# A graph network on one core: the first pass's register loads of slot numbers, in fours behind copies on ScalarE and in eights behind counts on TensorE

## The reference, cut to what matters

```python
h = jnp.maximum(_layernorm(x, axis=-1), 0.0)             # x: 6250 nodes x 128
h = _gcn_conv(h, src, dst, ones_e, W1, b1, n)            # 106250 edges, sorted by dst
h = h / jnp.maximum(jnp.sqrt(jnp.sum(h * h, axis=-1, keepdims=True)), 1e-12)
ev = _edge_encoder(h, src, dst, We1, be1)                # sigmoid(h[src] @ We[:H] + h[dst] @ We[H:] + be)
na = _node_encoder(h, src, dst, ev, Wn1, bn1, n)         # relu(segment_sum(ev * h[src], dst) @ Wn + bn)
ev2 = _edge_encoder(na, src, dst, We2, be2)
g = _node_encoder(na, src, dst, ev2, Wn1, bn1, n)
x = x + _gcn_conv(g, src, dst, ev2, W2, b2, n)
```

## Time and profile before

| | us |
|---|---|
| median of 3 runs | 3329.52 (3324.85 to 3332.83) |
| the profiled execution, its own time | 3348.71 |
| its span, first to last instruction | 3346.9 |
| first pass, from its first strip copy to the last | 143.3 to 977.1 |
| of it: before the first flush | 143.3 to 163 |
| of it: first stage, 27 turns, counts and pairs | 163 to 534 |
| of it: second stage, counts, pairs and pieces | 534 to 980 |
| TensorE's mean granted clock | 0.924 of full |

### The profile page before, as it was taken

The page is one execution under the profiler, slowest core; times in us unless marked ns, Lnnn a source line. Parts: engine busy times, 40 slices in busy tenths (PEclk is TensorE's granted clock), DMA queues, the critical chain, the costliest instruction groups (busy, mean ns, idle before and its releaser), DMA issues.

```text
span 3346.9 us, 58780 instructions
## 1 busy us (share of the span) xinstructions
PE 2635.7 (79%) x16470; PEld 2291.0 (68%) x16470; DVE 2111.6 (63%) x6199; ACT 1617.9 (48%) x3249; POOL 1866.2 (56%) x1816
## 2 busy tenths in 40 slices
PE   0667667898997677777789899999999676777775
PEld 0344446888885667666678788888888566666665
DVE  5567676665635566666675567666676456666667
ACT  7256565666666454554454444444444422233232
POOL 5345456555405666667720666666661267776673
PEclk9788898999999898988899899999999888888998
DMA  4244445555542333333322444444442433333333
GB/s 114 80 147 152 147 155 192 193 208 211 189 174 78 100 100 106 107 98 114 99 71 79 124 134 135 135 135 135 134 134 81 141 98 97 107 106 100 112 99 94
DMA packets 185594, 419.58 MB, mean 125 GB/s; under 512 B 36655, under 2 KB 136700, under 8 KB 175533
## 3 DMA queue, kind: packets, MB, share of 16 engines
q10 hardware_dynamic: 83703, 244.23, 20.6%
q0 software_dynamic: 61472, 140.49, 15.3%
q1 hardware_dynamic: 40118, 31.23, 3.0%
HBM read 311.35 MB, written 102.16 MB: 124 GB/s over the span
## 4 chain that ended last, share of the span: by engine, by line
PE 67%; issue 13%; DVE 9%; ACT 3%; ACTq 3%; another core or an unknown queue 2%; DMA 1%; DVEq 1%; POOL 1%; SPq 0%; POOLq 0%
PE ps L1117 18%; PE ps_high L1109 16%; PE ps_high L1117 12%; PE ps L1057 7%; PE ps_high L1075 3%; PE ps L1041 3%; ACT tab_area L769 2%; PE ps_high L1070 2%; ACTq L377 1%; PE ps_high L1196 1%; DVE acc L1592 1%; DVE tab_area L1521 1%; PE ps L1229 1%; DVE weights L1568 1%
## 5 line engine op out<-in xcount | busy, mean ns | idle before, releaser
L601 POOL DMA_INDIRECT rows<-table,edge_src x1664 | 1759.9, 1058 | 1164.0 <-SPq L496 604.0
L1109 PE MATMUL ps_high<-rows,weights 128*128 x2784 | 648.0, 342 | 385.2 <-issue 235.6
L1117 PE MATMUL ps<-tab_area,acc 128*128 128x129 f32 (+2 forms) x4410 | 824.2, 327 | 7.4 <-issue 6.1
L1109 PEld LDWEIGHTS ps_high<-rows,weights 128*128 128x128 f32 x2784 | 473.6, 204 | 486.9 <-issue 292.9
L1117 PEld LDWEIGHTS ps<-tab_area,acc 128*128 128x128 f32 x4410 | 698.6, 206 | 52.3 <-issue 7.2
L863 ACT ACTIVATE step<-xbuf,rows 128x128 f32 x928 | 358.0, 394 | 690.4 <-PE ps_high L1109 312.8
L1592 DVE TENSOR_TENSOR acc<-acc 128x640 f32<-128x640 f32 x735 | 604.9, 823 | 102.3 <-ACT acc L872 64.7
L1117 PE MATMUL ps_high<-tab_area,acc 128*128 128x129 f32 (+2 forms) x2940 | 588.3, 326 | 0.3 <-issue 0.3
L1575 DVE TENSOR_TENSOR acc<-acc,ps_high 128x129 f32 (+1 forms) x948 | 335.1, 354 | 384.9 <-PE ps_high L1109 187.8
L769 ACT ACTIVATE tab_area<-ps_high x816 | 404.4, 496 | 304.9 <-PE ps_high L1075 178.7
L1117 PEld LDWEIGHTS ps_high<-tab_area,acc 128*128 128x128 f32 x2940 | 478.0, 206 | 29.8 <-issue 1.2
(11 more groups left out here) (242 smaller groups left out, 2177.8 us busy)
## 6 DMA issues: line engine op xcount, KB each, us to landing
acc<-counts ACTq DMA_DIRECT2D x105, 1120.0 KB
counts<-tab_area ACTq DMA_DIRECT2D x51, 1568.0 KB
acc<-counts ACTq DMA_DIRECT2D x25, 1568.0 KB
rows<-table,edge_src POOLq DMA_INDIRECT x1664
table<-tab_area SPq DMA_DIRECT2D x6, 903.0 KB, 4.8
table<-acc SPq DMA_DIRECT2D x7, 448.0 KB, 4.2
table<-tab_area SPq DMA_DIRECT2D x6, 455.0 KB, 3.9
table<-tab_area SPq DMA_DIRECT2D x6, 448.0 KB, 3.0
```

What stands on the lines that cost most here:

```text
L601: nc.gpsimd.indirect_dma_start(rows[:, t % UNROLL, 0:row_floats[k]], None, tables[k], bass.IndirectOffsetOnAxis(ap=edge_src[:, t:t + 1], a ...
L1109: nc.tensor.matmul(ps[DENSE_BANKS + m % PAIR_BANKS][:, 0:WIDTH[k]], weights[:, m % W_RING, :], rows[:, bass.ds(known["slots"][m % UNROLL], ...
L1117: ins = nc.tensor.matmul(ps[j][:, 0:WIDTH[k]], gate_blocks[:, n % S_RING, j * PART:(j + 1) * PART], table[:, h, 0:WIDTH[k]], start=(h == 0 ...
```

## The change

ScalarE no longer loads 16 + 16 slot numbers at a flush. It loads 4 numbers of `done_from` behind the copy of each slot m with m % 4 = 0, and 4 of `count_to` behind that of m % 4 = 1, for the group of four slots that follows. The two numbers of a flush are loaded one behind the copy of the turn's slot 10 and one behind that of slot 11. At the flush itself only the wait for the last copy, the wait for the flush before and the DMA are left. TensorE loads 8 + 8 numbers in two instructions, one behind the counts of the third slot of each eight and one behind those of the seventh, for the next eight slots. The values, the copies, the matmuls and the DMAs are the same.

```diff
-        def load_slots(engine, table, i, top):
+        def load_some(engine, table, i, n, top):
             return nc.values_load_multi_w_load_instructions(
-                table[0:1, i * UNROLL:(i + 1) * UNROLL], engines=[engine], min_val=0, max_val=top,
+                table[0:1, i * n:(i + 1) * n], engines=[engine], min_val=0, max_val=top,
...
-            def slot_places(i):
-                return (load_slots(SCA, done_from, i, (REGIONS - 1) * REGION),
-                        load_slots(SCA, count_to, i, (C_RING - 1) * C_TILE // WINDOW + FLUSH - 1))
-
-            done_at, count_at = slot_places(0)
+            def load_done(i):
+                return load_some(SCA, done_from, i, QUAD, (REGIONS - 1) * REGION)
+
+            def load_count(i):
+                return load_some(SCA, count_to, i, QUAD, (C_RING - 1) * C_TILE // WINDOW + FLUSH - 1)
+
+            def load_flush(j, part, top):
+                return nc.values_load_multi_w_load_instructions(
+                    flush_to[0:1, j, part:part + 1], engines=[SCA], min_val=0, max_val=top,
+                    skip_runtime_bounds_check_because="a place in the ring and a tile")[1][0]
+
+            done_at, count_at = load_done(0), load_count(0)
             for m in range(QUAD * TURNS):
                 if m < SLOTS:
...
                     ins.then_inc(cells_copied, 1)
+
+                    if m % QUAD == 0 and m + QUAD < SLOTS:
+                        next_done = load_done(m // QUAD + 1)
+                    if m % QUAD == 1 and m + QUAD < SLOTS:
+                        next_count = load_count(m // QUAD + 1)
+                    if m % QUAD == QUAD - 1:
+                        done_at, count_at = next_done, next_count
+                    if m % FLUSH == FLUSH - 6:
+                        ring = load_flush(m // FLUSH, 0, C_RING - 1)
+                    if m % FLUSH == FLUSH - 5:
+                        tile = load_flush(m // FLUSH, 1, DENSE_TILES)
                     if m % FLUSH == FLUSH - 1:
                         j = m // FLUSH
-                        ring, tile = (nc.values_load_multi_w_load_instructions(
-                            flush_to[0:1, j, part:part + 1], engines=[SCA], min_val=0, max_val=top,
-                            skip_runtime_bounds_check_because="a place in the ring and a tile")[1][0] for part, top in ((0, C_RING - 1), (1, DENSE_TILES)))
-                        if m + 1 < SLOTS:
-                            done_at, count_at = slot_places(j + 1)
                         act.wait_ge(cells_copied, m + 1)
...
                 def count(m):
                     u, b = m % (2 * QUAD), m // QUAD
                     if u == 0:
-                        at = load_slots(TEN, cell_turns, m // (2 * QUAD), (REGIONS - 1) * REGION)
-                        first_pass.cell_at, first_pass.zero_at = at[:2 * QUAD], at[2 * QUAD:]
+                        first_pass.cell_at, first_pass.zero_at = first_pass.cells_next, first_pass.zeros_next
...
+                    if u == QUAD // 2 and m + 2 * QUAD < SLOTS:
+                        first_pass.cells_next = load_turn(2 * (m // (2 * QUAD) + 1))
+                    if u == QUAD + QUAD // 2 and m + 2 * QUAD < SLOTS:
+                        first_pass.zeros_next = load_turn(2 * (m // (2 * QUAD) + 1) + 1)
+
+                def load_turn(i):
+                    return load_some(TEN, cell_turns, i, 2 * QUAD, (REGIONS - 1) * REGION)
...
                 pe.wait_ge(ld_slot_rows, 16 * 6)
+                first_pass.cells_next, first_pass.zeros_next = load_turn(0), load_turn(1)
```

More of the change, by code:

```diff
@@ L768, in _ @@
                         act.wait_ge(cells_done, m)
[L769 to L770 removed]
+                    ins = act.activation(c_cells[:, bass.ds(count_at[m % QUAD], NODE_TILES, step=PART // WINDOW), :],
+                                         ps_high[:, bass.ds(done_at[m % QUAD], CELLS)].rearrange("p (h d) -> p h d", d=WINDOW), ACT.Copy)
                     if m > 0:
```

2 lines of the change are left out of this document (removed).

## The result

The changed kernel takes 3307.64 us (median of 5 runs, 3297.96 to 3309.3) where the kernel before takes 3329.52 (5 runs, 3324.85 to 3334.41): a ratio of 0.9932, with a 95% interval of 0.9916 to 0.9949. It is faster, by 22 us and not by the 47 that were forecast. The profiled execution took 3307.64 us, with a span of 3305.8 and a mean granted clock of 0.929. The profiled execution of before had been 19 us over its median, so the two spans differ by 41 us, of which 21 us lie behind the first pass, where nothing was changed.

The account below looks back on a forecast made before the run. ScalarE's flush stop was taken to hold up the first stage, TensorE to bound the second. Gains of 43 us (first stage), 2 (flush ahead) and 2 (second stage) summed to 47, giving 3282.5 us, range 3256 to 3313.

Parts of the forecast that it names:

- what bounds: First stage: no engine near full, waits in turns, ScalarE's flush stop among them; second stage: TensorE's own.
- the flush: ScalarE's stop at each flush falls from 2.96 to 0.75 us, 2.21 us shorter.
- what is late next: First stage: ScalarE's need nears VectorE's and TensorE's, so coupling waits don't shrink; 328 us, 43 less than 371.
- ScalarE's loads: New loads behind ScalarE's copies: four numbers take 0.43 us; uncovered 0.5 us a turn, plus 0.4 for flush traffic.
- the straight line: Price of a register load drawn between one and sixteen numbers, 0.049 us a number: four in a row 0.43 us.
- TensorE's loads: Two loads of eight at 0.66 us each fit under queued work; 8 us of first-stage stops go.
- The second stage gives 1 to 3 us: Second stage: small gain from clears waiting behind ScalarE's copies (2.0 us) and from issue (0.6 us).
- VectorE and the pairs take over: Rival: ScalarE's gain turns into TensorE's waits at groups VectorE marks late; gain 20 us, 3309.5 us; chance 0.20.
- The clock comes back too: Rival: fewer stops also restore part of TensorE's clock; gain about 70 us, 3259.5 us; chance 0.18.
- Short loads are not short: Rival: four in a row cost 1.00 us like four apart, so the kernel gets slower, 3410 us; chance 0.08.
- Nothing comes of it: Rival: the loads slow each other and use up the gain, within 7 us of before; chance 0.04.
- The signs named in advance: Checks on stop, load times, copy spacing, first stage about 45 us earlier, clock, and a chain without ScalarE's slot loads.

Follow-up runs that it names:

- c1: The kernel before, with waits against loaded numbers turned into waits against constants, but for one in sixteen: 0.9998 of the kernel before.
- c2: The whole change, with the same constant waits as c1: 0.9929 of the kernel before.
- d1: c1 with ScalarE loading in fours behind copies in the first stage only, TensorE's loads as before: 0.9863 of the kernel before.
- c3: c2 with TensorE's loads put back as before, so ScalarE's part of the change alone: 0.9905 of the kernel before.
- c4: c1 with TensorE's two loads of eight only, ScalarE's loads as before: 1.0018 of the kernel before.
- f1: The whole change, plus TensorE's and VectorE's pair loads split into fours and ones: 0.9888 of the kernel before.
- e2: ScalarE's part of the change, plus TensorE's and VectorE's pair loads split into fours and ones: 0.9817 of the kernel before.
- d2: c1 with ScalarE loading in fours behind copies in the second stage only, TensorE's loads as before: 1.0042 of the kernel before.
- d4: c3 without L371, TensorE's load of four numbers that lie four apart: 0.9760 of the kernel before.
- d3: c1 without L371, TensorE's load of four numbers that lie four apart: 0.9939 of the kernel before.
- e1: c3 with the four numbers of TensorE's load L371 copied once to neighbouring places: 0.9838 of the kernel before.
- f3: e2 with TensorE's slot numbers loaded in fours too: 0.9839 of the kernel before.
- e3: c3 with TensorE's 16 slot numbers still in one load, but behind the counts of each eight's seventh slot: 0.9952 of the kernel before.

## Why the prediction was right and wrong, by its steps

**The account in the sum's own terms**, before and after, by the two traces: ahead of the first stage 3 us came of the 2 forecast, in the first stage 26 of 43, and in the second 9 us were lost where 2 were to be gained. Together the pass ends 20 us earlier and not 47. In c1 and c2 the same terms are 4, 40 and a loss of 18. Which of the two stages missed more hangs on the pair of traces, but both missed.

**Right: what bounds, and the flush.** ScalarE's stop was on the path of the first stage. It fell from 2.96 to 0.68 us (forecast 0.75), and the change in the first stage by itself gave 44 us of the whole time (d1), where the sum had 43 for it and 2 for the flush ahead of it. The step "what is late next" held in its main point, that the waits which couple three nearly equal engines would not shrink.

**Mis-sized: ScalarE's loads.** Quiet they took 0.312 us and not 0.43. The cover was there. Before, the flush's first load began at 459.65 and the stop of 2.96 us ahead of the copy at 462.78 only at 459.82, so 0.17 of its 0.28 us ran under the last copy; behind each of the three loads lay a gap of 0.02 to 0.04 us. After, in the first stage, the copy behind a load of four under 0.4 us starts 0.528 us after the one before (median of 149), behind a load of one number (0.279 us) 0.528 (54), and with no load between 0.529 (162). So the uncovered 0.5 us a turn are zero. In the wake they took 0.9 to 1.1 us; 67 of the 216 in the first stage took over 0.4. The copy behind such a load follows in 1.06 us in the median (0.88 to 1.2 for the middle half), so 0.35 to 0.7 us each, 2.5 a turn: some 1.3 us a turn where I had 0.4. Both terms together were 0.9 and came out as 1.3, some 10 us over the stage. The prediction had the right reading at hand, "pieces of some 0.25 us, each holding a few neighbours", and chose the straight line beside it. By pieces the load of 16 pair numbers at 3.604 us is four pieces of 0.9 us, and the price of one piece in a wake could have been read before the result.

**Wrong: TensorE's loads.** The step said that a load of eight would be covered by what is queued, and that 8 us of stops would go. They did not. Of ScalarE's 120.8 us of idle time in the first stage after, 20.5 are the flush stops and some 35 the loads in a wake; the other waits are some 65 us, as much as the 63.5 before and not 8 less. With the loads in the wake that makes 20 us over the sum; 4 us less elsewhere leave the 16 by which 344 us lie over the 328 worked out (c2 and c3 had 332 and 333, from 372). In the whole time the part seems to cost 6 to 8 us (c3, c4, at the edge of noise), and 24 us where nothing else is long (f1 against e2, clear of it). The loads of 16 had stood at slots 0 and 8 of a turn. In the first stage 21 of those 54 were slow before; in the second stage one of 45. The "behind counts" of the change puts them to slots 2, 6, 10 and 14, and in the second stage 23 of 90 are slow (over 1.2 times the median). I had looked at what is queued ahead of a load and not at when in a turn it runs.

**Wrong: the second stage.** "The second stage gives 1 to 3 us" was the step that failed in its sign. It was right that nobody waits there for ScalarE's stop. But the stop also set when the flush's DMA goes out. With the stop, that DMA went out 1.8 us behind the last copy in this stage (2.5 us in the first); now it is 0.2 us. So in five of the 23 turns TensorE's pair loads, which had mostly begun just ahead of the flush, now run in its wake: in the kernel after L371 takes 2.6 to 3.7 us there where it mostly had 1.0, and with ScalarE's part alone (c3) L365 takes 4.0 to 4.2 and L371 another 1.5. The stage is 14 us longer in c3, 10 us when it alone is changed (d2, 13 us of the whole time), and 1 us with L371 gone (d4 against d3). In c3 half of the 14 us is TensorE standing longer (45.7 us against 38.9) and half is more busy time for the same work at a lower clock (395.4 against 388.2, 0.96 against 0.99). That the DMA's earlier issue moved the loads into the wake is read from the order in the traces; no run moved the DMA alone. The prediction noted L365 at 3.604 us, priced it for ScalarE's own loads, and didn't ask which of the loads that stay would meet the flush after the change. It also took TensorE's loads in this stage as covered, by the 0.6 us of "issue" ahead of the pieces. The pairs' matmuls, which stand behind the pair loads, already stood for 11.7 us there:

```profile
L1041 PE MATMUL ps<-rows,weights 128*128 x524 | 104.7, 282 | 25.2 <-issue 11.7 <-DVE weights L1500 10.7 <-DVE xbuf L1507 2.1
```

**Of the rivals**, none was the one. "VectorE and the pairs take over" has the time (3309.5 us forecast, 3307.64 measured) and one of its signs: VectorE's lines have 21% of the chain of the first stage, shown below, where they had 12%. Its mechanism isn't what was measured: ScalarE's other waits did not grow, in d1, with the same VectorE, the first stage keeps 38 us, and the loss of the second stage goes with one load. "The clock comes back too" came in a small part, 0.90 for 0.87 in the first stage, and was seen once L371 was gone or the pair loads were short: 0.97 in d4 and e2. The quarter of the stage at half clock, which its sum uses, no run shows as such; it is an estimate from the mean. The traces give the clock as a share of full speed: in that of before it was 0.50 from 464 to 467, behind that flush, and 1.00 from 468 to 470, and with these two levels a mean of 0.87 is 0.26 of the time at 0.50; the 0.90 of after is 0.20. "Short loads are not short" is refuted for quiet loads by the 0.312 us; in the wake, with 0.9 to 1.1, it holds for a third of those of the first stage. "Nothing comes of it" is out, as the gain is clear of noise. The chain of the first stage after:

```profile
by line: issue 16.4%; PE ps_high L1082 15.9%; PE ps_high L1087 15.0%; PE ps L1054 14.7%; ACT tab_area L776 10.0%; DVE tab_area L1541 9.1%; DVE tab_area L1538 4.8%; DVE xbuf L1527 4.5%; DVE weights L1520 2.8%; ACTq L377 2.7%; DVEq L365 1.2%;
```

**The signs named in advance:** ScalarE's stop, the loads of 0.3 us and of 0.5 to 0.7 for eight, the copies 0.53 us apart, the clock of the first stage and VectorE's share of the chain came as named. The first stage ended 29 us earlier and not 45, and the chain still holds ScalarE's loads, for 2.7% of the stage where it was 9.3%. The two that were named for failure both came: loads in the wake of 0.8 us or more on ScalarE, and a second stage that moves by more than 5 us.

## What to carry to other kernels

Four numbers four apart took 1.000 us to load here, and the same four side by side 0.333 (e1); sixteen in a row took 1.02 on ScalarE, and a load of four 0.312, under a copy of 0.497. So lay the numbers side by side, and try them in short loads, each behind work that covers it. This paid for ScalarE's slot numbers and for the pair loads, and it did not for TensorE's slot numbers (f3). Watch the loads where a large DMA takes data out of on-chip memory: there a load of four took 0.9 to 1.1 us instead of 0.31, while a read-back that filled the DMA engines as well left a load of eight at 0.592 us. When a stop on one engine goes, look at what that engine issues next to it: a DMA that went out 1.6 us earlier here met other work of another engine, in a stage where nobody had waited for the stop. Ask that of each load that stays, not only of those that are new.

## What the runs showed of the hardware

- A register load (TENSOR_LOAD) of one number took 0.28 us on ScalarE and 0.31 on TensorE (e2), of four in a row 0.31 and 0.33 (f3), of eight 0.59, of sixteen 0.97 (SyncE) to 1.11, and of four numbers four apart 1.00; the same four put in a row took 0.33 (e1). An estimate from these is a piece of four neighbours at some 0.25 to 0.33 us; how wide a piece is was not tried by itself.
- In the wake of a flush loads took some three times as long, by the same estimate 0.9 us a piece: mostly 0.9 to 1.1 us for four in a row (at most 1.6, in e3), 1.6 to 2.1 for eight (at most 2.5, in f1), up to 4.4 for four apart (e3) and 4.5 for sixteen (d2). It was so on four engines; at their worst, in the kernel after, ScalarE's four took 1.366 us, and sixteen 3.702 on VectorE, 3.600 on TensorE and 4.072 on SyncE (quiet 1.10, 1.10 and 0.97). The flush takes 1568 KB from on-chip to device memory. A read-back of as many bytes the other way, at a DMA share of 1.03 against 1.10, left a load of eight at its quiet 0.592 us, and of the 978 loads that began 5.7 to 9 us behind a flush in the second stages of the 17 traces none took over 1.2 times the median of its line. So in these traces it was the flush and not full DMA engines as such; why, no run shows. Outside a flush's wake a few loads were slow too, at the start of the pass and in the later passes (ScalarE's first of 16 at 140.9 us of the kernel before: 1.226 us, no flush issued yet; TensorE's 16 pair numbers, L365, at 1044.0 us of the kernel after, behind the last flush at 957.1: 1.831 us).
- A load on ScalarE's sequencer ran under the engine's copy of 0.497 us: with a load of 0.312 us between them the next copy started 0.528 us after the one before, without a load 0.529.
- TensorE's clock fell to 0.50 behind a stop of 3.78 us, on dense work (788.60 to 790.60 of the kernel after; 0.81 over the 7.4 us that followed the stop), and behind the stop of 4.58 us in c3 (0.50 from 522.30 to 526.00; 0.64 over 7.4 us), and the first stage's mean rose from 0.90 (c3) to 0.97 (d4) when L371 was gone. That took the shorter stops of ScalarE as well: with its stops as before the mean stayed low with L371 gone (0.85 in d3, 0.87 in c1).
